# A four-layer graph network on one core: a new hand-written order of the same pieces, nine steps deep instead of eight

## What is computed

```python
h = relu(layernorm(x)); x = x + L0(h, adj)   # 4 heads of attention over edges with adj > 0.5
h = relu(layernorm(x)); x = x + L1(h, adj)   # max over 7 relations: A, A^T, shift, shift^T, eye ...
h = relu(layernorm(x)); x = x + L2(h, adj)   # relu(D^-1/2 (A+I) D^-1/2 (h W + b))
h = relu(layernorm(x)); x = x + L3(h, adj)   # softplus(xn W_self + (I - S_out A S_in) xn W_neigh)

# L0: e = leaky_relu(e_dst[i] + e_src[j]), masked by adj > 0.5, softmax over j, times h
# L1: HW_r = h W_r + w_edges_r W'_r ; out = max_r(A_r HW_r) + b
```

## Time and profile before

| | us |
|---|---|
| runs | 712.42, 710.67, 710.19 |
| median | 710.67 |
| profiled execution | 712.24 |
| its span (first to last instruction) | 710.2 |
| PE busy in the span | 647.2 (91%) |
| DVE / ACT / POOL busy | 535.8 / 542.2 / 376.0 |

### The profile page before, as it was taken

The page is one execution under the profiler, slowest core; times in us unless marked ns, Lnnn a source line. Parts: engine busy times, 40 slices in busy tenths (PEclk is TensorE's granted clock), DMA queues, the critical chain, the costliest instruction groups (busy, mean ns, idle before and its releaser), DMA issues.

```text
span 710.2 us, 20332 instructions
## 1 busy us (share of the span) xinstructions
PE 647.2 (91%) x7476; PEld 522.0 (74%) x7476; DVE 535.8 (75%) x1641; ACT 542.2 (76%) x1271; POOL 376.0 (53%) x435
## 2 busy tenths in 40 slices
PE   5267999999999999999999999999999999999855
PEld 2164878778696968778696968778696978778544
DVE  3657888887978787887978787887978778595731
ACT  2487778888888889888888889888888896885442
POOL 1526566464937466464937466464936361474420
PEclk9679999999999999999999999999999999999986
DMA  6112140312212040212212040212212030200000
GB/s 208 49 44 68 70 135 2 90 63 77 75 54 98 4 148 3 91 61 77 76 54 98 3 149 3 93 60 77 75 52 85 4 134 2 77 2 1 16 15 16
DMA packets 39532, 44.47 MB, mean 63 GB/s; under 512 B 4545, under 2 KB 23050, under 8 KB 39434
## 3 DMA queue, kind: packets, MB, share of 16 engines
q1 hardware_dynamic: 38802, 42.95, 19.1%
q10 hardware_dynamic: 632, 0.22, 0.1%
HBM read 38.83 MB, written 4.33 MB: 61 GB/s over the span
## 4 chain that ended last, share of the span: by engine, by line
PE 79%; issue 6%; DVE 5%; ACT 4%; DMA 2%; SPq 1%; POOL 1%; ACTq 0%; POOLq 0%; DVEq 0%
PE ps L1763 13%; PE ps L1819 8%; PE ps L1910 7%; PE ps L1806 7%; PE ps L1961 7%; PE ps L1749 7%; PE ps L1856 5%; PE ps L1853 4%; PE ps L1854 4%; PE ps L1943 4%; PE ps L1855 2%; ACT y L692 2%; PE ps L1704 2%; PE ps L1894 2%; PE ps L1680 2%
## 5 line engine op out<-in xcount | busy, mean ns | idle before, releaser
L788 ACT ACTIVATE side<-d_all,sd 128x512 bf16<-128x512 f32 x256 | 163.8, 711 | 28.2 <-DVE pos L1268 19.9
L477 POOL TENSOR_TENSOR rstd<-ve,half_neg 128x4 f32<-128x4 f32 (+1 forms) x67 | 90.3, 1347 | 159.0 <-DVE ve L1349 70.6
L1268 DVE TENSOR_TENSOR pos<-side,none 128x2048 bf16<-128x2048 bf16 x64 | 79.9, 1249 | 41.1 <-ACT side L788 36.0
L1763 PE MATMUL ps<-part,pos 128*128 128x66 bf16 x3072 | 103.2, 193 | 3.3 <-DVE pos L1268 3.3
L1763 PEld LDWEIGHTS ps<-part,pos 128*128 128x128 bf16 x3072 | 100.0, 97 | 6.2 <-DVE pos L1268 3.8
L1330 DVE TENSOR_REDUCE best<-ps 128x128 f32<-128x896 f32 x64 | 68.0, 1082 | 3.2 <-PE ps L1857 3.2
L1749 PE MATMUL ps<-part,nmask 128*128 128x66 bf16 x1536 | 54.8, 197 | 15.8 <-DVE part L1257 15.8
L1749 PEld LDWEIGHTS ps<-part,nmask 128*128 128x128 bf16 x1536 | 52.5, 99 | 19.8 <-issue 19.6
L1961 PE MATMUL ps<-u,adj_tr 128*128 128x128 f32 x512 | 62.9, 283 | 2.5 <-ACT u L888 2.5
L536 POOL TENSOR_TENSOR val<-hv,val 128x512 f32<-128x512 f32 x32 | 35.2, 1121 | 55.3 <-ACT val L754 55.3
L1961 PEld LDWEIGHTS ps<-u,adj_tr 128*128 128x128 f32 x512 | 60.3, 197 | 3.7 <-ACT u L888 3.7
(11 more groups left out here) (162 smaller groups left out, 1507.4 us busy)
## 6 DMA issues: line engine op xcount, KB each, us to landing
adj_in<-in_adj SPq DMA_DIRECT2D x16, 1024.0 KB, 5.4
d_all<-d_dram SPq DMA_DIRECT2D x64, 256.0 KB, 3.8
x_in<-in_x SPq DMA_DIRECT2D x16, 256.0 KB, 2.9
out_y<-y_out SPq DMA_DIRECT2D x15, 256.0 KB, 2.3
d_dram<-sd_t SPq DMA_DIRECT2D x64, 2.0 KB, 1.4
w_sb<-in_L_gnn_W SPq DMA_DIRECT2D x7, 64.0 KB, 2.5
b_sb<-in_L_gnn_b SPq DMA_DIRECT2D x1, 256.0 KB, 3.5
out_y<-y_out SPq DMA_DIRECT2D x2, 128.0 KB, 1.8
```

What stands on the lines that cost most here:

```text
L477: G.tensor_tensor(rstd[:, cut], ve[:, cut], half_neg[:, cut], ALU.pow).then_inc(power, 1)
L788: last = A.activation(side[:, t, :], d_all[:, h, :], ACT.Sign, bias=sd[:, 0, h, t:t + 1])
L1268: V.tensor_tensor(pos[h % 2][:], side[:], none[:], ALU.is_gt).then_inc(pos_ok, 1)
L1763: last = mm(ps[:, B_HEADS[q] + i // 2, o:o + VAL], pos[h % 2][:, t, i * P:(i + 1) * P], parts[n][:, t, h, :], start=False, stop=(i % 2 == ...
```

## The change

The same pieces are issued, with the same instructions, in another order on every engine and on SP's DMA queue. DEPTH is 9 instead of 8; the loop starts at s = 7 instead of 6 and makes 10 rounds instead of 11. The PSUM banks are dealt out anew, and PE's waits for free banks with them. In the prologue the scores' DMAs stand ahead of loads and of the edge rows, and `set_up` stands behind the first transposes and projection. `degrees` on POOL, `add_bias` and the norms stand elsewhere too. In the tail `relation` of graph 14 is interleaved with the heads of graph 15. The core of the diff (the orders of POOL, and the rest of prologues and epilogues, are left out):

```diff
-DEPTH = 8
+DEPTH = 9
-B_ADJ = (3, 6, 2, 4)
-B_H0T, B_PROJ = 0, 0
-B_HEADS = (4, 2)
-B_SUMS, B_H1T, B_AH, B_ATH = 7, 6, 7, 5
-B_REL = (2, 4, 6, 2)
-B_LIN, B_LAP = 7, 6
+B_ADJ = (5, 2, 5, 2)
+B_H0T, B_PROJ = 0, 6
+B_HEADS = (4, 0)
+B_SUMS, B_H1T, B_AH, B_ATH = 1, 0, 3, 2
+B_REL = (2, 0, 2, 4)
+B_LIN, B_LAP = 3, 2
...
@@ SP queue @@
             load_laplace()
+            scores_out(at(0))
+            load_features(at(2))
+            scores_in(at(0))
+            load_features(at(3))
             load_edge_rows()
-            scores_out(at(0))
-            scores_in(at(0))
-            load_features(at(2))
-            load_features(at(3))
...
-            for s in range(8, GRAPHS + 5):
+            for s in range(8, GRAPHS + 6):
                 load_features(at(s))
+                store(up_to_last(s - 6))
+                load_adjacency(at(s - 2))
                 scores_out(at(s - 2))
                 scores_in(at(s - 2))
-                store(up_to_last(s - 5))
-                load_adjacency(at(s - 1))
...
@@ PE: prologue @@
-            set_up()
+            broadcast_rows()
             adjacency(0)(at(0))
-            broadcast_rows()
             h0_transposed(at(0))
             adjacency(1)(at(0))
+            adjacency(2)(at(0))
             project(at(0))
+            adjacency(3)(at(0))
             mean_value(at(0))
             top_rows(at(0))
-            adjacency(2)(at(0))
             top_all(at(0))
-            adjacency(3)(at(0))
+            set_up()
+            h0_transposed(at(1))
+            project(at(1))
+            row_sums(at(0))
             no_edges(0)(at(0))
...
```

More of the change, by code:

```diff
@@ L609, in _ @@
[L609 to L614, removed]
+            rstd_0(at(4))
+            add_b1(at(0))
+            own_blocks(at(0))
+            rows_without_edges(0)(at(1))
+            degrees(at(1))
+            rstd_2(at(0))
+            rows_without_edges(1)(at(1))
+            add_bias(at(3))
+            rstd_1(at(1))
+            values(at(2))
@@ L977, in _ @@
-            sums_across(at(2))
+            sides(3)(at(2))
             z_transposed(at(0))
-            sides(3)(at(2))
+            row_sums(at(3))
             laplace_in(at(0))
             laplace_own(at(0))
-            row_sums(at(3))
             hidden2(at(1))
+            projected(at(3))
+            adjacency(0)(at(3))
             h2_transposed(at(1))
-            adjacency(0)(at(3))
-            for s in range(6, GRAPHS + DEPTH - 1 - 6):
-                projected(at(s - 3))
[L988 to L1013, removed]
-                laplace_own(at(s - 5))
-                h2_transposed(at(s - 4))
-                adjacency(0)(at(s - 2))
@@ new lines, in _ @@
+            adjacency(1)(at(13))
+            softplus(at(10))
+            conv_in(at(11))
+            adjacency(2)(at(13))
+            weights(at(13))
+            adjacency(3)(at(13))
+            hidden1(at(12))
+            part_hi(at(13))
+            sides(0)(at(13))
+            part_mid(at(13))
+            conv_relu(at(11))
+            h0_transposed(at(15))
+            sides(1)(at(13))
+            product_ath(at(12))
+            low_weights(at(13))
+            product_ah(at(12))
@@ L1522, in _ @@
-                weights(at(s - 3))
-                node_scales(at(s - 4))
+            largest(1)(at(11))
+            pair(0)(at(12))
+            head(2)(at(12))
+            largest(2)(at(11))
+            largest(3)(at(11))
+            head(3)(at(12))
+            residual1(at(11))
+            norm2(at(11))
+            pair(1)(at(12))
+            scores(at(13))
+            attention(at(12))
+            laplace(at(10))
+            top_score(at(13))
+            residual0(at(12))
+            norm1(at(12))
@@ L1989, in _ @@
             adjacency(2)(at(1))
+            adjacency(3)(at(1))
+            top_rows(at(1))
             top_all(at(1))
-            adjacency(3)(at(1))
-            h0_transposed(at(2))
+            project(at(2))
+            h0_transposed(at(3))
+            mean_value(at(2))
             product_ah(at(0))
+            product_ath(at(0))
+            row_sums(at(1))
             h1_transposed(at(0))
-            product_ath(at(0))
+            no_edges(0)(at(1))
             relation(0)(at(0))
+            head(0)(at(1))
@@ new lines, in _ @@
+            head(3)(at(12))
+            laplace_product(at(10))
+            adjacency(0)(at(13))
+            h2_transposed(at(11))
+            top_rows(at(13))
+            adjacency(1)(at(13))
+            adjacency(2)(at(13))
+            conv_bias(at(11))
+            top_all(at(13))
+            adjacency(3)(at(13))
+            conv_linear(at(11))
+            h0_transposed(at(15))
+            project(at(14))
+            conv_product(at(11))
+            product_ath(at(12))
+            row_sums(at(13))
@@ L2076, in _ @@
[L2076 removed]
+            project(at(15))
             adjacency(3)(at(14))
             conv_product(at(12))
[L2079 removed]
+            h1_transposed(at(13))
+            product_ah(at(13))
             product_ath(at(13))
[L2081 to L2084 removed]
+            no_edges(0)(at(14))
+            row_sums(at(14))
+            head(0)(at(14))
             relation(0)(at(13))
```

769 lines of the change are left out of this document (417 added, 352 removed).

## The result

The changed kernel takes 700.29 us (median of 699.71, 701.95 and 700.29) against 710.67: the ratio is 0.9848, 95% interval 0.9827 to 0.9869. Four more runs of it beside other kernels gave 700.06. It is faster, by 10.4 us in the medians.

What follows compares the result with a forecast made beforehand. PE, busy 647.2 of 710.2 us, was taken as the floor, leaving 63 us idle to cut. Gains of 9.3 (loop), 5.5 (head) and 1.9 (tail) sum to 16.7 us: 710.67 to 694.0 us, range 686 to 706.

Steps and rivals of the forecast that it cites:

- the forecast case: Whole kernel: loop, head and tail gains together give about 689 to 699 us; chance 0.60.
- rival 3: Head: gains nothing because its later waits (46 to 56, 82 to 88 us) are twice those reckoned; 699.5 us, chance 0.10.
- The loop: Ten rounds: both PE gaps covered, step 39.94 to 39.0 us, gain 9.3 us, between 0 and 10.5.
- rival 4: Whole kernel: new gaps just replace the old ones everywhere; 710 us, chance 0.04.
- The margin of `hidden1`: Loop: `product_ah` needs `hidden1`; PE's 6.88 us and short pieces against 6.8 on DVE and ACT leave about 0.5 us.
- rival 1: Loop: softplus and `hidden1` chain 0.5 to 1 us longer than reckoned, step not shortened; 703.3 us, chance 0.18.
- rival 2: Loop: POOL holds DVE by the port lock in each step, 2.2 us lost per step; slower, 714.9 us, chance 0.08.
- The head up to the first product: Head: scores ready near 15.8, `d_all` landing near 22.5, first product 6.9 us earlier; PE idle 25.9 to about 14.8.
- The head behind it: Head after the first product: waits of 11.6 us where 6.1 before, loss 5.5; whole head gains 5.5, between 0 and 9.
- The tail: After the loop: 3.3 us gained in steps 13 to 15, 1.8 to 2.2 lost later; net gain 1.9, bounds -2 and 4.
- Steps 13 to 15: Tail: gaps of 5 to 5.5 us before shrink to about 2.2, a gain of 3.3 us.
- The 0.4 for `laplace_own`: End of the tail: `laplace_own` of the last half now precedes the last softplus, worth 0.4 us.

Runs made afterwards that it cites:

- the kernel whose clock stays at 1.00: Changed kernel plus 12 unread TensorE products in the holes of the head; 698.75 us, ratio 0.9827, beside the changed kernel's 700.06.
- the run that counted them as one pass: Changed kernel plus 24 unread f32 128x512 products in the holes of the head; 699.66 us, ratio 0.9844.

## Why the prediction came near, and where it was off

Forecast 694.0 with a range of 686 to 706; measured 700.3. It is faster and inside the range, but a little outside the 689 to 699 that I called the forecast case, and close to the 699.5 of rival 3, whose condition (a head that gains nothing) isn't met: that nearness is luck. In the medians the gain is 10.4 us where 16.7 was forecast. Of the 6.3 between them, 2.1 come from which executions were profiled (12.5 us in the span, 10.4 in the medians), and 4.2 are misses of the sum: the loop gave 1.3 more, the head 2.7 less and the tail 2.8 less.

- **The loop** was right, step and cause: 38.88 for 39.0, gain 10.6 for 9.3, so rival 4, new gaps for old ones, falls. The estimate of 38.9 without gaps, from start-to-start distances instead of listed durations, holds to 0.02. The margin of `hidden1` was put at 0.5 and measured as 0.53 in the trace, 0.3 to 0.4 by delay. So rival 1 was wrong, but by a margin that one copy of 0.6 us uses up.
- **POOL holding DVE** (rival 2) didn't come: `gl` takes 0.87 us where it took 2.42. The 64 `gl` instructions of the changed kernel take 278 to 284 ns each, where the slowest before took 1180. No run here made POOL and DVE meet badly in the new order, so the price of the rival stays untried.
- **The head up to the first product** was right: scores ready at 15.63 (15.8), `sides(0)(0)` at 22.64 (22.5 for the landing), first product at 31.92 in this profile, 31.5 to 33.2 in the others with the same order there (32.8). The run with the set-up products in front shows one part at work, for 4.1 us; what the place of the scores ahead of the edge rows is worth no run shows by itself.
- **The head behind it** is the first term that was mis-sized: the head as a whole gains 2.8 us instead of 5.5, although the first product came 0.9 earlier than forecast. I had put the waits behind the first product at 11.6 us. In the kernel whose clock stays at 1.00 PE does 55.4 us of the kernel's work between 32 and 102 us (60.21 busy less 4.79 of unread products), so it stands free for 14.6. In the changed kernel the listed waits sum to 9.7 only, because pieces at the lower level fill part of the same holes: PE is busy 60.2 us there. That is why its idle time up to the rounds even fell by more than the 5.6 forecast, from 32.0 to 25.1 us, while the same pieces took 4.1 us more of busy time, a price that the sum has nowhere. The clock isn't what the head fell short by, though: in the kernel with 12 products, at 1.00, the rounds start no earlier (115.59 against 115.03). Which of the chained durations was short I can't name from the record of the sum; the trace shows the chain of the scores of graph 1 behind the edge rows as the one that ends last near 50 us, and no run moves it.
- **The tail** is the second: -0.9 instead of +1.9. Steps 13 to 15 are the miss. From the second cut to the end of the last head it is 124.76 us against 127.41, of which 2.0 are pieces that the new order has elsewhere (`laplace_linear(13)` 1.8, and the small ones): a gain of 0.6 where I had 3.3. Their new waits are 0.53, 1.75, 0.97 and 0.33 = 3.6 us of idle time, 4.2 with the 0.16 that each costs besides, where I had 2.2. The old ones are 4.3 us in seven waits, 5.4 with the 0.16, inside my 5 to 5.5; the longest, in PE's timeline of the kernel before:

```profile
600.98 1.62 PE L1763 MATMUL ps<-part,pos 128*128 128x66 bf16 x48 [1.13 <-DVE pos L1268]
```

  That accounts for 2.1 of the 2.7; the other 0.6 stay open. From the end of the last head to the first relation it is 21.1 us (628.59 to 649.67), inside the 21 to 22 forecast; less the 1.8 of `laplace_linear(13)` the loss is 1.4, a little under my 1.8 to 2.2, of which the sum had taken the lower end. The 0.4 for `laplace_own` came as 0.3: from the end of the last `laplace_product` to the end of the span it is 5.61 us instead of 5.94. It doesn't show in the total (48.03 us from the first relation to the end, against 47.99) because that product started 0.1 later and took 0.27 longer.
- **The lower clock at the very end** was there before as well and is in no term; PE's timeline of the kernel before shows it in its last two pieces:

```profile
694.08 3.75 PE L1943 MATMUL ps<-w_both,zt 128*128 128x256 f32 x8 [0.75 <-ACT zt L878]
698.55 5.71 PE L1961 MATMUL ps<-u,adj_tr 128*128 128x128 f32 x32 [0.72 <-ACT u L888]
```

  It is a gain that neither order took; only the 0.27 us by which `laplace_product` differs (5.71 and 5.98) are part of the miss.

## What to carry to other kernels

Lay a new order out with start-to-start distances and look for the smallest margin; in this loop, where PE never waits, that gave the step to about a tenth of a microsecond, and a deliberate delay on the chip measures the margin. Waits in a pipeline's start or end are another matter: take one away and ask which is next, since here the removed wait of 1.75 us came back as 0.42 + 0.44 + 0.90. In this kernel a low granted clock cost time only where the slowed engine was what the next piece waited for, so look for the last work of the kernel before looking for the longest slow stretch.

## What was unexpected in the hardware

A low clock was free in one place and cost up to 3.9 us in another. In the head of the fitted kernel (granted clock 1.00 against 0.71 to 0.95 in 40 to 60 us) no gain could be told; at the end two pieces at the lower level, 3.75 + 5.98 us, became 1.97 + 3.84.

The clock also falls at different places in different executions of one order: `laplace_product` of the last graph took 5.98 and 5.46 us in the two profiles of the changed kernel, 3.84 in five others whose PE program is the same there, and 6.18 and 6.28 in two more. This, with the 49.9 to 51.7 us in the head, is enough to account for the 698.3 to 702.0 us of its executions, though no run isolates it.

An unread 128x512 product in f32 costs 0.87 us, since it runs as two passes of 0.45 each (12 passes in 5.32 us); the run that counted them as one pass overran its holes and lost what it had gained.
